# A recurrence between two FFN stages: VectorE's loop written out, and both FFN stages rearranged

## What is computed

```
x = x + attention(layernorm(x))            # 16 heads, 8 segments
x = x + ffn(layernorm(x))                  # FFN 1
x = x + recurrence(layernorm(x))
x = x + ffn(layernorm(x))                  # FFN 2

def ffn(x):                                # w_up 1024x256, w_down 256x1024, ternary
    h = gelu(rms_norm(x) @ w_up.T)
    return rms_norm(h) @ w_down.T

def step(state, (r, k, v, w, a, kk)):      # 512 steps, state 8 x 16 heads x 16 x 16
    sa = einsum(state, -kk)
    state = w * state + sa * (kk * a) + k * v
    state = state / (sqrt(mean(state ** 2)) + 1e-5)
    return state, sum(state * r)
```

## Time and profile before

| what | before |
|---|---|
| median of the runs | 2644.86 us |
| the profiled execution, measured | 2637.25 us |
| its span, first to last instruction | 2634.0 us |
| busy share of the span: TensorE, VectorE, ScalarE, GpSimd | 74%, 83%, 61%, 34% |
| attention, to the first up projection | 480 us |
| FFN 1, eight groups | 480 to 660 us |
| recurrence, eight stretches of 64 steps | 768 to 2378 us |
| FFN 2, eight groups | 2447 to 2634 us |
| mean granted TensorE clock, share of full speed | 0.807 |

### The profile page before, as it was taken

How to read it: one execution, slowest core, us unless ns; L and a number is a source line. 1 busy time by engine, 2 the same in 40 slices (tenths; PEclk the granted TensorE clock), 3 DMA queues, 4 the chain that set the end, 5 groups by cost and what they waited for, 6 DMA issues and landing times.

```text
span 2634.0 us, 52211 instructions
## 1 busy us (share of the span) xinstructions
PE 1948.5 (74%) x12353; PEld 1563.6 (59%) x12353; DVE 2193.4 (83%) x8801; ACT 1612.9 (61%) x5207; POOL 907.4 (34%) x1522
## 2 busy tenths in 40 slices
PE   5888887788688768777768787777886764345687
PEld 3555554445577767677667676677776763233454
DVE  6888777687239999999999999999999999992576
ACT  4888777566355565556666666666665554443566
POOL 0000000111025555555555555555555555550111
PEclk7999899899887787687887778877777776665799
DMA  5001000000000000000000000000000000000000
GB/s 170 16 20 27 20 16 12 1 1 1 1 0 1 1 1 1 1 1 1 1 1 1 1 1 1 1 1 1 0 0 1 1 1 1 1 1 0 9 25 33
DMA packets 14327, 24.52 MB, mean 9 GB/s; under 512 B 1280, under 2 KB 12032, under 8 KB 13824
## 3 DMA queue, kind: packets, MB, share of 16 engines
q1 hardware_dynamic: 14080, 21.97, 2.9%
HBM read 12.27 MB, written 4.19 MB: 6 GB/s over the span
## 4 chain that ended last, share of the span: by engine, by line
DVE 53%; issue 21%; PE 17%; ACT 8%; DVEq 1%; DMA 0%; POOL 0%; SPq 0%; ACTq 0%; POOLq 0%
DVE pn L1447 11%; DVE bank L1463 10%; DVE U L1504 7%; DVE xs L1435 4%; DVE bank L1452 4%; DVE kv L1496 4%; PE bank L248 3%; ACT prob L828 3%; PE bank L543 2%; PE bank L260 2%; PE bank L590 1%; DVE bank L1493 1%; DVE bank L1472 1%; PE bank L770 1%; PE bank L692 1%
## 5 line engine op out<-in xcount | busy, mean ns | idle before, releaser
L1581 POOL TENSOR_TENSOR wu<-U,stg 128x256 f32<-128x256 f32 x512 | 317.7, 620 | 761.3 <-DVE U L1504 761.3
L707 PE MATMUL bank<-U,ident 128*128 128x128 f32 x2080 | 470.3, 398 | 86.4 <-ACT go L969 72.0
L707 PEld LDWEIGHTS bank<-U,ident 128*128 128x128 f32 x2080 | 432.5, 235 | 124.5 <-issue 51.5
L770 PE MATMUL bank<-stack,tm 128*128 128x64 f32 x1792 | 325.3, 365 | 183.4 <-ACT tm L906 183.2
L770 PEld LDWEIGHTS bank<-stack,tm 128*128 128x128 f32 x1792 | 314.3, 276 | 204.2 <-issue 204.2
L1108 ACT ACTIVATE xs<-U 128x128 f32<-128x128 f32 x1024 | 262.3, 302 | 261.5 <-DVE U L1504 258.7
L1447 DVE TENSOR_REDUCE pn<-xs 128x16 f32<-128x256 f32 x1024 | 377.7, 409 | 7.3 <-issue 6.7
L1036 ACT ACTIVATE small<-pn 128x16 f32<-128x16 f32 x513 | 110.9, 216 | 371.3 <-DVE pn L1447 371.3
L1537 POOL TENSOR_TENSOR kv<-stg 128x256 f32<-128x256 f32 x513 | 317.4, 619 | 0.0
L1435 DVE TENSOR_TENSOR xs<-U,bank 128x128 f32<-128x128 f32 x1024 | 243.2, 278 | 67.6 <-issue 66.9
L1463 DVE TENSOR_TENSOR bank<-wu,bank 128x128 f32<-128x128 f32 x1024 | 292.2, 286 | 1.0 <-POOL wu L1581 0.7
(11 more groups left out here) (180 smaller groups left out, 3722.4 us busy)
## 6 DMA issues: line engine op xcount, KB each, us to landing
out_x<-x SPq DMA_DIRECT2D x8, 512.0 KB, 2.9
x<-in_x SPq DMA_DIRECT2D x1, 3584.0 KB, 16.9
Vs<-V SPq DMA_DIRECT2D x8, 384.0 KB, 4.6
Vs<-V SPq DMA_DIRECT2D x8, 288.0 KB, 3.3
lane<-in_lanes SPq DMA_DIRECT2D x8, 256.0 KB, 3.3
wcat<-in_wcat SPq DMA_DIRECT2D x1, 1792.0 KB, 14.0
wraw<-in_w_up SPq DMA_DIRECT2D x1, 1024.0 KB, 19.0
wraw<-in_w_down SPq DMA_DIRECT2D x1, 1024.0 KB, 11.4
```

What stands on the lines that cost most here:

```text
L707: last = pe.matmul(rsum.rearrange("p (t i) -> p t i", i=HD), ident[:, :], steps[:, :, :, j], start=(j == 0), stop=(j == HD - 1))
L770: last = pe.matmul(bank[3 + g][:, e * CH:(e + 1) * CH], tm[:, g * (PB // 2) + e, :, :].rearrange("p a c -> p (a c)"), stack[:, :], start=T ...
L1581: pool.tensor_tensor(ij(wu[:, :]), ij(U[:, half if j else 1 - half, (j - 1) % STEPS, :]), col(stg[:, half, j, TW, :]), ALU.mult).then_inc( ...
```

## The change

It has two parts.

VectorE's two loops of the recurrence become Python loops, so that its program for 64 blocks of eight steps and for the stretches without steps is straight code, and t0, it and m are constants. ScalarE, GpSimd and TensorE keep their loops.

In both FFN stages the preparation of the next group is put elsewhere. Statistics and moments are made two groups ahead (n = 1, 2 and 3), with those of the second group ahead of the stage's loop, or, for FFN 1, in the last batch of attention at w = 16 and 17. Scales and the four normalised rows stand at n = 0, TensorE's transposes at n = 2 and 3, ScalarE's splits at 3 and 4, VectorE's at 4 and 5, each with half k = 1 ahead of half k = 0. add_rows takes one, two and one tile at n = 4, 5 and 6. GpSimd's roots follow that order.

```diff
@@ ffn_pe
-                    pe.wait_ge(F["sr"], q if q % B == 0 else q - 1)
-                    pe.wait_ge(F["lo"], (q - 1) * KD + k + 1)
+                    pe.wait_ge(F["sr"], q if q % B == 0 else q - 1 if k == 0 else q - 2)
+                    pe.wait_ge(F["lo"], q * KD - k)
...
-            for k in range(KD):
+            for k in (1, 0):
                 rows_transposed(i * B, k)
...
-                    if n in (4, 5) and q < i * B + B - 1:
-                        rows_transposed(q + 1, n - 4)
+                    if n in (2, 3) and q < i * B + B - 1:
+                        rows_transposed(q + 1, 3 - n)
@@ ffn_act
-                act.wait_ge(F["xt"], q * KD + k + 1)
+                act.wait_ge(F["xt"], q * KD + 2 - k)
...
-                    if n in (5, 6) and q < i * B + B - 1:
-                        split_high(q + 1, n - 5)
+                    if n in (3, 4) and q < i * B + B - 1:
+                        split_high(q + 1, 4 - n)
@@ row_stats
-        def row_stats(dve, q):
+        def row_stats(dve, q, us=range(NT)):
@@ ffn_dve
-            for k in range(KD):
+            for k in (1, 0):
                 split_low(q0, k)
+            if not beside_first:
+                row_stats(dve, q0 + 1)
+                row_moments(dve, q0 + 1)
...
                     if q < q9:
                         if n == 0:
-                            row_stats(dve, q + 1)
-                            row_moments(dve, q + 1)
-                        if n == 2:
                             row_scales(dve, q + 1)
-                        if n in (2, 3):
-                            rows_normalised(dve, q + 1, (2 * n - 4, 2 * n - 3))
-                        if n in (6, 7):
-                            split_low(q + 1, n - 6)
+                            rows_normalised(dve, q + 1, range(NT))
+                        if n in (4, 5):
+                            split_low(q + 1, 5 - n)
+                    if q + 1 < q9:
+                        if n in (1, 2):
+                            row_stats(dve, q + 2, (2 * n - 2, 2 * n - 1))
+                        if n == 3:
+                            row_moments(dve, q + 2)
...
-                        if n in (4, 5):
-                            add_rows(q - 1, (2 * n - 8, 2 * n - 7))
+                        if n in (4, 5, 6):
+                            add_rows(q - 1, ((0,), (1, 2), (3,))[n - 4])
@@ ffn_pool
             row_roots(q0)
+            row_roots(q0 + 1)
             for q in range(q0, q9 + 1):
-                if q < q9:
-                    row_roots(q + 1)
                 if q > q0:
                     output_roots(q - 1)
+                if q + 1 < q9:
+                    row_roots(q + 2)
@@ VectorE, last_batch
+                if w == 16:
+                    row_stats(dve, 1)
+                if w == 17:
+                    row_moments(dve, 1)
@@ VectorE, recurrence
                 if not running:
-                    with dve.Fori(0, NB) as m:
+                    for m in range(NB):
...
-                with dve.Fori(0, NB // 2) as pair:
+                for pair in range(NB // 2):
                     for half in range(2):
                         m = pair * 2 + half
-                        t0 = dve.snap(n * CH + m * STEPS)
-                        it = dve.snap(n * NB + m)
+                        t0 = n * CH + m * STEPS
+                        it = n * NB + m
```

More of the change, by code:

```diff
@@ L311, in ffn_act @@
                     act.activation(hsq[:, t % 2, :], h[:, t % 2, :], ACT.Square).then_inc(F["sq"], 1)
-                    if n in (5, 6) and q < i * B + B - 1:
-                        split_high(q + 1, n - 5)
-        def row_stats(dve, q):
+                    if n in (3, 4) and q < i * B + B - 1:
+                        split_high(q + 1, 4 - n)
+        def row_stats(dve, q, us=range(NT)):
             dve.wait_ge(F["xn"], q * NT)
-            for u in range(NT):
+            for u in us:
                 dve.bn_stats(st[:, u, :], x[:, tile(q, u), :]).then_inc(F["bs"], 1)
@@ L347, in split_low @@
             def split_low(q, k):
-                dve.wait_ge(F["hi"], q * KD + k + 1)
+                dve.wait_ge(F["hi"], q * KD + 2 - k)
                 dve.tensor_tensor(xh[:, q % 2, 1, k, :], bank[k][:, :], xh[:, q % 2, 0, k, :], ALU.subtract).then_inc(F["lo"], 1)
```

## The result

The change makes the kernel 4.5% faster. The runs of the kernel after took 2520.36 to 2523.96 us, with a median of 2523.5; those of the kernel before took 2640.54 to 2644.88 us beside them, with a median of 2643.12. The ratio is 0.9546, with a 95% interval of 0.9529 to 0.9562.

What follows compares the result with a forecast made beforehand. It took VectorE, idle at loop jumps while targets were refetched, to bound the recurrence, and a border chain the FFN. Recurrence -70 and FFN -24 made -94, from the median 2644.86 to 2551 us, range 2524 to 2583.

Steps and rivals of the forecast that it cites:

- the price of a group of the FFN: FFN stages: a four-tile group takes 19.9 us in FFN 1 and 19.4 in FFN 2, bounds 18.6 and 20.8.
- the clock's 6 us given back: FFN stages: half of 12.3 us of lowered-clock time added back, since TensorE still idles in short pieces: +6.
- Recurrence, forecast 70.5: VectorE's recurrence: the idle gaps at 24 loop jumps go whole, -70.5 us, with bounds -47 and -77.
- The term for straight code: VectorE's recurrence: some 96 packet crossings cost the same 6 us as before, bounds 0 and 29 us.
- The other engines' jumps: Recurrence: ScalarE, GpSimd and TensorE keep their loops, and nothing of theirs takes the place of VectorE's gap.
- FFN, forecast 24: Both FFN stages: -16.8 and -14.4, +6 for the clock, +1.1 at attention's end; -24 us, bounds -45 and -2.
- The end of attention: Before FFN 1: group 1's statistics and moments, moved ahead of the last normalise, add 1.1 us.
- FFN all the way: Rival, FFN stages: 18.6 us a group with the clock staying up, -45 and -72, about 2528 us; chance 0.12.
- FFN stays bound: Rival, FFN stages: lateness only moves and the lowered clock stays, FFN -5 to -10, about 2567 us; chance 0.22.
- Exposed jumps of the other engines: Rival, recurrence: ScalarE's jump goes through whole in 24 places; recurrence -30, FFN -24, 2591 us; chance 0.05.
- Straight code that isn't fetched ahead: Rival, VectorE's recurrence: every crossing costs 2.80 us like a jump's target, slower at about 2820 us; chance 0.03.
- loops that cost nothing: Rival, recurrence: "issue" was something else, so removing loops gives 0, FFN -24, 2621 us; chance 0.02.

Runs made afterwards that it cites:

- The last kernel: The changed kernel with read_sums ahead of the statistics, FFN 2's add_rows one place later, FFN 1's second-group statistics out of attention; 2514.21 us, 0.9526 of before.
- e_ffn: The changed kernel with VectorE's recurrence loops put back, so the FFN rearrangement alone; 2601.8 us, ratio 0.9875 to before.
- e_late: The changed kernel with FFN transposes back at places 4 and 5, ScalarE's splits at 5 and 6, VectorE's at 6 and 7; 2554.31 us, 0.9676 of before.
- e_align: The kernel before with satisfied waits ahead of VectorE's eight loops, so every body begins at the block place of n = 5; 2583.24 us, ratio 0.9806.
- e_shift: The kernel before with 40 always satisfied wait instructions once ahead of VectorE's whole recurrence; 2637.28 us in one run.
- e_fill: The kernel before with eight matmuls that nobody reads at each border between FFN groups; 2629.42 us, ratio 0.995.
- r_after: The changed kernel run again unaltered, beside three others on one chip; 2524.11 us, ratio 0.9555 to before.
- e_all: The changed kernel with the loops of ScalarE, GpSimd and TensorE written out as well; 2524.72 us, ratio 0.956 to before.
- e_best: The changed kernel with three moves in VectorE's FFN program (read_sums, add_rows, second-group statistics); 2514.21 us, ratio 0.9526 to before.
- the first run: The kernel before with only VectorE's recurrence loops written out, both FFN stages as before; 2559.9 us, ratio 0.9717.

## Why the prediction was wrong

The mechanisms were right and their sizes weren't. The forecast took 94 us out of the span, and 112.3 went. What failed are the price of a group of the FFN (8.7 us), the clock's 6 us given back, the gaps of the recurrence (7.4: 4.0 for those that straight code was to keep, 3.4 for what a gap costs beyond its idle time) and the base that the difference was taken from (7.6).

**What bounds the kernel: right.** "Issue" was the refetch at a jump. Moving a body to another place in its block of 128 instructions makes it come or go, with the loop untouched.

**Recurrence, forecast 70.5, measured 77.9.** The 24 jumps went, as worked out. The term for straight code was mis-sized: I kept the 6.3 us of short gaps, and the view shows 2.3 us, 0.03 for each of VectorE's 85 packets. That makes 74.5. The other step that failed is that I took a gap's price for its idle time. VectorE was busy for 1526.0 us of its recurrence before and 1522.3 after, with the same 7144 instructions. They didn't get shorter. In the records of VectorE an instruction starts some 0.08 us before the one ahead of it has ended, as in after

```profile
1502.19 0.48 DVE L1513 TENSOR_TENSOR U<-bank,kv 128x128 f32<-128x128 f32 x2
1502.59 0.47 DVE L1444 TENSOR_TENSOR xs<-U,bank 128x128 f32<-128x128 f32 x2
```

and ahead of a gap that overlap is missing, as in before, where the product of 1523.63 in the earlier trace rows follows

```profile
1520.35 0.48 DVE L1504 TENSOR_TENSOR U<-bank,kv 128x128 f32<-128x128 f32 x2
```

From start to start the first takes 0.40 us and the second 3.28, which is 2.88 more for a gap of 2.80. There are 58 gaps for issue before and 10 after; 48 times 0.08 are 3.9 us. With them the sum is 78.4, and small things elsewhere take 0.5 back. My bound of 77 was 1 us short, because it counted idle time alone.

**The other engines' jumps: right.** GpSimd waited 760.3 us for VectorE's sum before and 683.3 after, 77 us less. Its loop had room, as the earlier trace rows had it.

**FFN, forecast 24, measured 38.2.** The mechanism was right (the late splits made the border, the border lowered the clock), and three sizes were off.
1. The clock, 6 us. I gave half of the 12.3 us back for TensorE's short idle times. The filler run puts its worth at 12.4 us, and after gives none of it back. The reason that I named had no row; the quick group of the earlier trace rows had such short idle times too, and a clock of 0.97.
2. The price of a group, 8.7 us in fourteen of them. I took 18.6 with all hidden, as 17.4 from the last group plus two sets of transposes in full. (The 15.36 us for seven intervals make 17.6 for eight, so the 17.4 was 0.2 too low besides.) The last kernel shows 17.81 with all preparation done, so the transposes lie for the most part in TensorE's gaps. Against that the lateness was 1.22 a group (0.44 and 0.78), where I had 0.5 and 0.3. Together that is 19.03 against 19.4. I also took one price for all seven intervals. The first group of each stage has none before it to finish and takes 17.31 us, 2.6 and 2.1 less than I had; the last interval of each is 19.35 and 18.59, since the group after next isn't there to prepare.
3. The end of attention, +1.8 in place of +1.1. It is two steps of nearly the same size. VectorE's last normalise comes 0.91 us later behind the moved statistics, where I had 1.1. Then the four projections that it feeds run at a lower clock. In after they stand in the timeline as

```profile
478.64 0.42 DVE L1231 TENSOR_TENSOR oT_a<-bank,rdT 128x256 f32<-128x256 f32 x1
...
479.12 2.08 PE L632 MATMUL bank<-wo_a,oT_a 128*128 128x256 f32 x4 [1.04 <-DVE oT_a L1231]
```

where before has, right behind the normalise of the earlier trace rows,

```profile
474.08 1.22 PE L627 MATMUL bank<-wo_a,oT_a 128*128 128x256 f32 x4 [0.61 <-DVE oT_a L1226]
```

That is 0.86 us more for the same four matmuls, at a granted clock of 0.50 (479.0 to 481.2) against 0.86 (474.0 to 475.4). The moved instructions explain this second step only in part. In e_ffn and e_late the clock is still 1.00 when rdx, the last copy ahead of them, is made, and falls as far behind it as in before; there the later start puts the projections into the lowered stretch (2.08 us). In after it had fallen before the statistics began (0.50 from 476.4 us on), as it had in e_align, e_shift and e_fill, whose attention ends with the code of before and whose projections take 2.08 us too. So part of the 0.86 is that the profiled execution of before was a good one here. With the statistics put back, as in the last kernel, the normalise has its 1.00 us of idle time again.

**Attention itself, not forecast.** The other 4.1 us of the +5.9 lie ahead of the moved code: rdx stands at 472.31 in before and 476.44 in after. In r_after it stands at 480.20, in e_all at 474.98, in e_best at 470.94, with the same instructions up to there. So attention's length differs from one execution to another by some 9 us, more than any term of the FFN's sum that was off.

**From the span to the median, 7.6 us.** The profiled execution of before (2637.25) was a quick one, 7.6 us under the median of 2644.86 that the forecast started from, while that of after is at its median (2523.96 against 2523.5). I subtracted a difference worked out from the one from the median of the others. Such a median is no firm base either: in the later sets before has 2635.77, 2641.69 and 2641.39. An attention that was short in the profiled execution would explain the 7.6, and the clock in FFN 1 can move a run by 3 us, but the slower runs of before have no trace here, so this is argued and not shown. The forecast is above the median of after by 27.5 us: 18.3 in the terms above (7.9 recurrence as against the 70 of the sum, 14.2 FFN and attention's end, less 4.1 of attention, and 0.3 rest), 7.6 here, and some 1.6 that lies outside the span or between the run and its median.

**The rivals.** FFN all the way (2528) came nearest, with 45 us for the FFN where 38.2 were measured. It went wrong by the price of a group too, as its 18.6 was no bound. That FFN stays bound (2567) fell with the windows. Exposed jumps of the other engines fell with the run that wrote them out. Straight code that isn't fetched ahead (2820) fell with 0.03 us a packet, and loops that cost nothing (2621) with the first run. The range ended 0.5 us too high at its low end. It should have gone down to the sum of my own bounds (2523) and past it, as the profiled execution of before was known to be 7.6 us quicker than its median.

## What to carry to other kernels

When an engine idles at the jump of a long hardware loop and the trace shows instruction packets there, the price is a property of where the body stands. It can be had back by writing the loop out or, in part, by moving it, and it is a little more than the idle time listed; a loop on an engine with room is not worth touching. A late operand at a border costs twice where TensorE idles over it, once as the wait and once as the lower clock behind it: a few matmuls that nobody reads measure the second part by itself. And price a pipelined stage by its first, its middle and its last group; here the first and the last made 6.0 of the 8.7 us by which fourteen groups were off.

## What the runs showed of the hardware

- The instructions of VectorE, ScalarE and GpSimd come in packets of 8.2 KB (1.15 MB in 140). Where no other engine's packet falls between, VectorE's straight code in after takes one every 127 to 130 instructions, about 18 us here, at 0.03 us of idle time each. A jump whose target had to be fetched cost 2.8 to 4.1 us and five packets, one whose target was there 0.3 to 0.4 and none.
- A pair of n = 5 is 376 instructions in the trace, waits and jump counted. In its first pass packets start beside its 4th, 129th and 257th instruction (three more start beside the 72nd, 223rd and 317th in e_shift too, where the body is moved by 40, so they are another engine's), so its body begins at a packet's edge and fits three. Shifted by 40 it fetched 5 packets in a pair. The body of n = 4 has 368 instructions, and in its second to fourth pass packets start at the 115th or 116th and the 242nd, so it begins 14 behind an edge and also spans only three, and yet its jumps were the dearest. It ends two instructions short of its third block where n = 5 ends eight short. That a fetch ahead of the end throws out the first block would explain both, but no run here tried it by itself.
- The Trainium skill, in "Runtime: NRT & Kernel Launch", section Instruction fetch mechanics, has an instruction memory of 32 KiB in two blocks of 16 KiB (256 instructions). The packets of these three engines are half that, 8.2 KB; those of q8, which rose from 11 to 42 when TensorE's loop was written out, have 16.4 KB. As an estimate from the page's 32 KiB, four packets of 8.2 KB would fit, and three blocks and one fetched ahead, as in n = 5, agree with that, where two blocks of 256 would hold the body and no fetch ahead. No run here shows the size of the memory.
- A stall of VectorE costs some 0.08 us more than the idle time that the profile lists, because the overlap of two instructions is lost with it: with 58 gaps for issue before and 10 after, the recurrence's busy time went from 1526.0 to 1522.3 us with the same instructions.
- TensorE's granted clock fell to its lower level behind idle times of 2.3 us, and four matmuls of 512 columns took 1.86 us there in place of 1.03. Behind other idle times of the same length it stayed up.
